# Merged semaphore clears, an earlier second-to-last expert, and context loads in four parts, in a decoder kernel of two layers

## What is computed

```
x = x + xattn0(layernorm(x), ctx, mask)     # keys with mask == 0 are left out
x = x + ffn0(layernorm(x))                  # self attention over 1024 rows, gate, top-2 router,
                                            # 8 experts 256->512->256 with a norm and gelu inside
x = x + xattn1(layernorm(x), ctx)
x = x + ffn1(layernorm(x))                  # 8 experts, each takes its 512 best of 4096 tokens;
                                            # y = W2 (silu(W1 x) * (W3 x)) * weight, added into x
```

## Time and profile before

| | us |
|---|---|
| median of 3 runs | 1932.36 (1932.31 to 1933.12) |
| the profiled execution | 1935.92 |
| its span, first to last instruction | 1934.2 |

### The profile page before, as it was taken

One profiled execution on the slowest core, in us unless ns is written; L12 is line 12 of the kernel. 1 busy time (PEld: TensorE's weight loads), 2 busy tenths in 40 slices (PEclk: granted clock), 3 DMA queues, 4 the chain that ended last, 5 costly groups with the idle time before them and its releaser, 6 DMA issues. The chain is left out here.

```text
span 1934.2 us, 29342 instructions
## 1 busy us (share of the span) xinstructions
PE 1684.8 (87%) x10227; PEld 790.7 (41%) x10228; DVE 1232.6 (64%) x2122; ACT 972.6 (50%) x1811; POOL 578.7 (30%) x637
## 2 busy tenths in 40 slices
PE   6899799899999999999999793999458996529996
PEld 4466464222222222222222472577334664225564
DVE  6444358788888888888882386566484554671221
ACT  3432245488888888888888220344275331202220
POOL 5200063243221211121112135466565000104433
PEclk9999999899999999999999895899779998759998
DMA  5000059632222222322200622122310000612542
GB/s 147 1 2 1 20 171 301 220 78 41 40 40 40 40 40 49 61 48 40 40 2 2 233 72 85 53 67 67 117 42 1 1 2 1 224 66 69 129 98 33
DMA packets 112770, 134.72 MB, mean 70 GB/s; under 512 B 18576, under 2 KB 88592, under 8 KB 112368
## 3 DMA queue, kind: packets, MB, share of 16 engines
q1 hardware_dynamic: 101920, 114.33, 21.9%
q0 software_dynamic: 9552, 17.97, 3.9%
q10 hardware_dynamic: 1152, 0.54, 0.1%
HBM read 78.60 MB, written 54.06 MB: 69 GB/s over the span
## 5 line engine op out<-in xcount | busy, mean ns | idle before, releaser
L1070 DVE TENSOR_REDUCE sa_mhalf<-sa_a 128x2 f32<-128x1024 f32 x512 | 604.1, 1220 | 84.7 <-PE sa_a L1282 82.8
L1215 ACT ACTIVATE sa_e<-sa_b 128x512 f32<-128x512 f32 x683 | 383.9, 602 | 77.1 <-PE sa_b L1315 77.1
L1325 PE MATMUL sa_b2o<-sa_e,sa_v 128*17 128x512 f32 x2048 | 269.7, 598 | 0.0
L1215 ACT ACTIVATE sa_e<-sa_b2o 128x512 f32<-128x512 f32 x341 | 205.4, 602 | 40.7 <-PE sa_b2o L1315 40.7
L1315 PE MATMUL sa_b<-sa_q,sa_k 112*128 112x512 bf16 x468 | 163.4, 388 | 2.7 <-ACT sa_e L1215 2.7
L1018 POOL TENSOR_TENSOR sa_rden<-sa_o_rows,sa_minus_one 128x16 f32<-128x16 f32 x32 | 93.0, 2907 | 178.3 <-ACT sa_o_rows L1198 178.3
L234 DVE TENSOR_REDUCE xa_mx<-xa_rows 128x16 f32<-128x1024 f32 x64 | 78.3, 1224 | 96.5 <-PE xa_rows L603 96.2
L1282 PE MATMUL sa_a<-sa_k,sa_q 48*128 48x512 bf16 x704 | 113.4, 389 | 13.2 <-DVE sa_mhalf L1070 13.2
L1007 POOL CAST sa_negm<-sa_neg 16x128 bf16<-16x128 f32 x32 | 9.4, 292 | 348.8 <-issue 339.0
L478 ACT ACTIVATE xa_pT<-xa_cols 128x1024 f32<-128x1024 f32 x64 | 62.1, 1021 | 82.5 <-PE xa_cols L635 82.5
L1315 PEld LDWEIGHTS sa_b<-sa_q,sa_k 112*128 112x128 bf16 x468 | 40.6, 97 | 151.3 <-ACT sa_e L1215 129.7
(11 more groups left out here) (344 smaller groups left out, 2950.0 us busy)
## 6 DMA issues: line engine op xcount, KB each, us to landing
k_parts<-sa_parts SPq DMA_DIRECT2D x96, 128.0 KB, 2.2
tc_w<-in_L_ffn_W SPq DMA_DIRECT2D x24, 512.0 KB
sa_q<-q_parts SPq DMA_DIRECT2D x44, 192.0 KB, 5.4
sa_k<-k_parts SPq DMA_DIRECT2D x44, 192.0 KB, 5.8
q_parts<-sa_parts SPq DMA_DIRECT2D x16, 384.0 KB
ex_xg<-expert_in SPq DMA_DIRECT2D x39, 132.0 KB
v_groups<-sp_vt SPq DMA_DIRECT2D x8, 544.0 KB, 4.7
sa_v<-v_groups SPq DMA_DIRECT2D x16, 272.0 KB, 7.4
```

The source lines that it names most:

```text
L1070: nc.vector.tensor_reduce(mhalf[a % 2][:, half, head:head + PAIRED + 1:PAIRED, t], aps[a_slot(use)][:], axis=X, op=ALU.max).then_inc(a_use ...
L1215: nc.scalar.activation(ex[(KT * n + kt) % (LAG + 1)][:, head], bps[use % 3], ACT.Exp, scale=SCALE).then_inc(b_used, 1)
L1325: last = nc.tensor.matmul(ops[32 * head:32 * head + VW], vs[s][:, kt, head], ex[(KT * n + kt) % (LAG + 1)][:, head], start=(kt == 0), stop ...
```

## The change

1. A `Kit` can be given a keeper: its semaphores' numbers go into the keeper's list and it opens no clearing block of its own. `xa0_` gives its to `c0_`, `sa_` to `sp_`, `ex_` to `at_`, `xa1_` and `c1_` to `sm_` (the scope around the self-attention layer), `sw_` and `tc_` to `x_`. `ao_`, `ts_` and `ct_` keep their own. Lists are sorted before they are cleared.
2. A context's loads: the keys' weights, the four context loads, the values' weights, the queries' weights, the two other biases; later the output's weights and `bo`. Keys, values and queries get semaphores of their own, and TensorE waits for each where it is used. In the first cross attention the mask goes behind x chunk 3 instead of behind chunk 7, and DVE's key bias, values and fill are moved. In the first cross attention, too, scores of the first chunk start one iteration earlier.
3. Expert tiles: `add_b2` runs two tiles ahead instead of one.
4. Closing experts: the outputs of expert 6 are made, weighed and scattered behind block f = 1 of expert 7's `hidden`; SP, not GpSimd, waits for the last scatters.

```diff
 class Kit:
-    def __init__(self, nc, ctx, prefix):
+    def __init__(self, nc, ctx, prefix, keeper=None):
         self.nc, self.ctx, self.prefix = nc, ctx, prefix
-        self.numbers = []
-        ctx.callback(self.clear_semaphores)
+        self.numbers = keeper.numbers if keeper else []
+        if not keeper:
+            ctx.callback(self.clear_semaphores)
...
+        self.numbers.sort()
         with self.nc.Block() as block:
...
     def issue(self, sp):
         w = self.w
-        loads = [(self.wts[:], w["wts"].rearrange("f (k p) n -> p f k n", p=P))]
...
+        def weights(f):
+            return self.wts[:, f], w["wts"][f].rearrange("(k p) n -> p k n", p=P)
...
+        self.keys_count = load(self.keys_loaded, weights(1), *[(self.ctxT[:, k, :, twice, :], w["ctxT"][k * P:(k + 1) * P])
+                                                               for twice in range(2) for k in range(HALVES)])
+        self.values_count = load(self.values_loaded, weights(2))
+        self.queries_count = load(self.queries_loaded, weights(0))
+        self.count = load(self.loaded, (self.bqk[:], w["bqk"]), (self.bv[:], w["bv"].partition_broadcast(P)))
+        self.issued = True
+
+    def issue_output(self, sp):
+        w = self.w
+        for dst, source in ((self.wts[:, 3], w["wts"][3].rearrange("(k p) n -> p k n", p=P)),
+                            (self.bo[:], w["bo"].partition_broadcast(P))):
             sp.dma_start(dst, source).then_inc(self.loaded, 16)
+        self.whole = self.count + 32
...
                         if c == 4:
                             context.issue(sp)
+                            context.issue_output(sp)
...
                         if c == 0:
                             context.issue(sp)
-                    sp.dma_start(mask_i[:], mask.rearrange("(t p) k -> p t k", p=P)).then_inc(mask_loaded, 16)
+                        if c == 3:
+                            sp.dma_start(mask_i[:], mask.rearrange("(t p) k -> p t k", p=P)).then_inc(mask_loaded, 16)
+                    context.issue_output(sp)
...
                     moments(1)
-                    place_key_bias()
                     for c in range(CHUNKS):
                         if c >= 1:
                             normalize_x(c)
-                        if c == 0:
-                            place_values()
                         if c + 2 < CHUNKS:
                             moments(c + 2)
+                        if c == 0:
+                            place_key_bias()
                         if c == 2:
+                            place_values()
+                        if c == 3:
                             place_fill()
...
-                pool.wait_ge(context.loaded, context.count)
+                pool.wait_ge(context.loaded, context.whole)
...
-                    act.wait_ge(kbias_made, 1)
                     act.wait_ge(k_psum, HALVES)
...
                         evacuate_qT(c, half)
+                    if c == 0:
+                        act.wait_ge(kbias_made, 1)
...
-                pe.wait_ge(context.loaded, context.count)
+                pe.wait_ge(context.keys_loaded, context.keys_count)
...
+                pe.wait_ge(context.values_loaded, context.values_count)
...
+                pe.wait_ge(context.queries_loaded, context.queries_count)
...
-                        if c >= CHUNKS - 2:
+                        if c >= CHUNKS - 3:
                             pe.wait_ge(qT_ready, HALVES)
-                            scores(0, c - (CHUNKS - 2))
-                    scores(0, 2)
+                            scores(0, c - (CHUNKS - 3))
                     scores(0, 3)
...
+                pe.wait_ge(context.loaded, context.whole)
                 for c in range(CHUNKS):
                     attend(c)
...
                 def body(k, turn, j, ahead):
-                    if k + 1 < MT:
-                        add_b2(k + 1, turn + (j + 1) // U, (j + 1) % U)
+                    if k + 2 < MT:
+                        add_b2(k + 2, turn + (j + 2) // U, (j + 2) % U)
...
+                add_b2(1, 0, 1)
                 turns(pool, body)
...
                     load(sp, e + 3, e % 3)
+                sp.wait_ge(scattered, 16 * CAPT * E8)
...
-                pool.wait_ge(scattered, 16 * CAPT * E8)
...
+                        if f == 1 and e + 1 == E8:
+                            outputs(e - 1)
...
-                for e in range(1, E8):
+                for e in range(1, E8 - 1):
                     hidden(e)
                     outputs(e - 1)
+                hidden(E8 - 1)
                 outputs(E8 - 1)
...
+                        if f == 1 and e + 1 == E8:
+                            weigh(e - 1)
...
-                for e in range(1, E8):
+                for e in range(1, E8 - 1):
                     gate(e)
                     weigh(e - 1)
+                gate(E8 - 1)
                 weigh(E8 - 1)
```

More of the change, by code:

```diff
@@ L84, in __init__ @@
     def __init__(self, kit, w):
-        self.w, self.loaded, self.issued = w, kit.sem("loaded"), False
+        self.kit, self.w, self.loaded, self.issued = kit, w, kit.sem("loaded"), False
+        self.keys_loaded, self.values_loaded, self.queries_loaded = (kit.sem(f"{n}_loaded") for n in ("keys", "values", "queries"))
         self.wts = kit.sb("wts", [P, 4, HALVES, D])
@@ L2501, in _, with swiglu_experts @@
                 dve.wait_ge(inverted, 1)
-def swiglu_experts(nc, ident, weights, load, w_loaded, idx, less_best, rz, gathers, x_stored, out):
+def swiglu_experts(nc, keeper, ident, weights, load, w_loaded, idx, less_best, rz, gathers, x_stored, out):
     with ExitStack() as ctx:
-        kit = Kit(nc, ctx, "sw_")
+        kit = Kit(nc, ctx, "sw_", keeper)
         sb, ps, sem = kit.sb, kit.ps, kit.sem
```

34 lines of the change are left out of this document (17 added, 17 removed).

## The result

The changed kernel took 1919.62 us (median of 4 runs, 1912.33 to 1922.00) beside 1932.74 us of the kernel before: a ratio of 0.9923, 95% interval 0.9898 to 0.9948. It is faster by 13.1 us, where 26.5 us were forecast, and 13.7 us above the forecast time.

A forecast was written before the change was run, and what follows sets the result against it. TensorE, busy 87%, was taken to bound the long stages, leaving only its holes and the boundaries; 10.3 + 9.3 + 1.0 + 1.9 + 4.0 = 26.5 us, taken from the profiled time and then 3.6 for the median, gave 1905.9 us, range 1900 to 1915.

The forecast's parts named there:

- clears and blocks: Stage boundaries: sorted, shared lists merge semaphore clears into ranges and drop six clearing blocks; 10.3 us less, bounds 8 and 11.3.
- start-up: First cross attention: reordered loads start keys and chunk 1 earlier, scores one iteration earlier; 9.3 us less, bounds 5 and 12.
- second cross attention: Its reordered loads sit behind five row loads and TensorE waits for ACT's rows anyway; 0 us, bounds -1 and +1.
- expert tiles: End of that loop: the last addition one body earlier lets GpSimd's scatters close up; 1.0 us less, bounds 0 and 2.
- closing scatters: Closing stage: expert 6's outputs inside expert 7's products let the last scatter start earlier; 1.9 us less, bounds 1.0 and 2.9.
- drain: Kernel's end: with SP waiting, GpSimd's drain ends 3.3 us behind the last scatter, not 7.3; 4.0 us less, bounds 0 and 5.1.
- Rival (a): Boundaries: clears don't merge because living semaphores' numbers lie between; only blocks go, 2.0 us instead of 10.3, giving 1914; chance 0.11.
- The mask's term: First cross attention: the 1 MB mask ahead of x chunks 4 to 7 delays chunk 4; -1.5 us, bounds 0 and -4.
- rival (b): Start-up held by loads: quarters pay fixed parts, keys land no earlier than 13.97; 5.7 us instead of 9.3, 1909.5; chance 0.12.
- Rival (c): Kernel's end: GpSimd's drain takes as long as it did; 4.0 us less gain, giving 1910; chance 0.11.
- the sign that I had set for it: Kernel's end: GpSimd's drain ending 5 us or more behind the last scatter's end, instead of 3.3, would show Rival (c).
- (d): Self-attention or closing stage: new timing lowers TensorE's clock; slower needs 53 us more low stretches, mean under 0.93; chance 0.03.

The follow-up runs named there:

- number 3: The kernel before with only the changed loads of the two contexts, their waits, and DVE's and TensorE's order in start-up: 1925.83 us (5 runs), ratio 0.9959.
- number 8: The changed kernel with the last wait for the scatters' landing on GpSimd again instead of SP: 1918.35 us (4 runs), ratio 0.9929.

## Why the prediction was wrong

**By its terms.** Measured is the difference of the means over all traces with and without the edit:

```
term                      forecast   measured
clears and blocks           10.3       9.6    (14.6 - 5.0; number 3 has 14.8)
start-up                     9.3       8.4    (233.4 in 5 traces, 225.0 in 12)
second cross attention       0        -4.4    (241.4 in 4 traces of it without the edit or hold;
                                               245.3, 249.6, 241.3, 247.0 of the changed kernel)
expert tiles                 1.0       1.8    (177.1 in 6, 175.3 in 11)
closing scatters             1.9       1.7    (190.3 in 5, 188.65 in number 8)
drain                        4.0       2.3    (188.65 in number 8, 186.3 in 10)
sum                         26.5      19.4
```

The remaining four stages add 0.4 or less either way. Over four occasions the kernel before had medians of 1932.2 to 1933.8 us and the changed one 1919.6, 1917.5, 1911.8 and 1913.5; all 16 runs of it have a median of 1914.9, some 18 us below before.

**Clears and blocks: right.** I counted 8 clears in 8 blocks and there are 14, with the long ranges at 0.18 to 0.37 us: 0.7 us less. Rival (a) is out.

**Start-up: right in place, and in size partly by luck.** Keys at 11.46 (forecast 11.7), chunk 1's transposes at 18.31 (19.4), transposed maxima at 67.07 (65.4) instead of 74.73; the stage 9.3 us shorter in the trace after and 8.4 in the mean. Up to the maxima the gain was 7.7 us, not 9.3. By TensorE's chunks it is 7.5 for the start of chunk 1 (forecast 6.4) and 3.0 for its work at 2.4 GHz (3.0), then -4.0 for the mask (-1.5): 2.3 us of them until chunk 3 starts, and 1.7 for its projection, 5.29 us instead of 3.60 at the lower clock. One round less behind the loop, with its products inside it, gives 1.2 (1.4). The mask's term was thus the mis-sized one; the last 1.6 us of the stage's 9.3 came behind the maxima, where the trace of before has 3.4 us at 1.2 GHz, from 76.2 on, and the trace after none. The three transfers more didn't run one by one, so rival (b) is out: the second x landed at 13.61 (forecast 13.5) instead of 15.44. The Trainium skill's wish for transfers of at least 1 MiB ("DMA: Bandwidth & Descriptors", section "Bandwidth") had no price here that the trace shows; the page's figures are for loads that GpSimd issues, and these are SyncE's. The part of the term that the clock gives back is not sure: the 12 traces lie between 222.5 (0 us at 1.2 GHz) and 226.5 us (6.8).

**Second cross attention: the step that failed.** "I take 0; bounds -1 and +1" looked only at what the edit does to this stage's loads. But two engines stood within 0.3 us of each other there: copy at 1469.31, first addition at 1469.57, as the rows above show, and I hadn't read them. In their place the runs showed a hold of two VectorE operations that costs the stage 3.1 to 4.6 us, in three of four traces of the changed kernel, and in the mean of the four, with the clock's own scatter in it, 4.4 us. Which side an execution falls on hangs on the clock of the projection ahead and, at 5.3 us, on the last 0.3 us. The price was there to be read too, in the start-up of the trace of before, where the last normalization stands beside the same additions:

```profile
39.45 1.34 DVE L224 TENSOR_SCALAR xa_xn<-x_x,xa_mv,xa_rstd 128x256 f32<-128x256 f32 x4
...
43.72 18.93 POOL L373 TENSOR_TENSOR x_x<-x_x,c_bo 128x1024 f32<-128x1024 f32 x8
47.22 8.60 DVE L224 TENSOR_SCALAR xa_xn<-x_x,xa_mv,xa_rstd 128x256 f32<-128x256 f32 x4 [0.89 <-PE xa_front L569]
```

Four instructions, 8.60 us instead of 1.34. A bound of one or two additions, 2.3 to 4.6 us, would have followed from it.

**Expert tiles: right in size.** The 1.8 us contain time at 1.2 GHz: the two slowest traces without the edit, 178.5 and 178.6 us, have 18 us of it. Of the traces without the edit, four have 12.3 to 12.5 us of it and took 176.2 to 176.4 us; with the edit it is 11.1 to 11.8 us and the stage 174.9 to 175.6. That is 1.0 us, of which up to 0.5 is still the clock's. The edit wasn't run by itself.

**Closing stage: the order right, the drain mis-sized.** The reordering gave 1.7 of 1.9 us. The drain ends 5.0 us behind the last scatter, not 3.3: the row that I took (the expert tiles) was the nearest of its kind and still another case. The 4.94 us that the drain took by itself in the closing stage was the row to use: 7.3 - 4.9 = 2.4. Rival (c), that nothing is gained, is out too, although the sign that I had set for it, a gap of 5 us or more, is met: the sign was wrong, since the gap was 7.3 us before.

**From the profile to the median: a constant that isn't one.** I forecast 1909.4 us for a profiled execution and 1912.33 was measured, 2.9 off, while the median was 13.7 off. I had taken the 3.6 us between the profile of before and its median over to the changed kernel, whose profile lay 7.3 us under its median. The near hit of the profile is luck: a slow draw of before against a fast one of after. Taking over the 3.6 us is the same as taking 26.5 us from the median of before, so it is no cause of its own. The 13.7 us are 26.5 - 19.4 = 7.1 in the terms above, the largest being the second cross attention; 1919.6 - 1914.9 = 4.7 between the first four executions, whose median is the highest of four occasions, and all 16; and 1.9 that the traces don't account for.

The kernel before scatters over 1928 to 1938 us, the changed one over 1907 to 1922, and the granted clock goes with it (0.943 at 1907.5, 0.936 at 1921.0). Two things are seen to differ between its four traces: the hold, which three have and one hasn't, and the stretches at 1.2 GHz, 218 to 233 us in total inside the stages. Which of them takes an execution to 1922 isn't shown: the three above 1918 us have no trace.

**The range.** The bounds of the parts, added up, are 13.0 and 34.3 us, not the 17 to 31 that I wrote and took 1900 to 1915 from. The 13.1 us measured lie at their very edge.

**Slower, by the clock (d):** no; the clock rose from 0.936 to 0.941.

## What to carry to other kernels

When an edit shifts a stage in time without touching it, look in that stage for a VectorE copy or other small operation on SBUF that starts within a few tenths of a microsecond of a long GpSimd operation, and price the other order. Here a GpSimd addition of 2.3 us beside a copy of 0.25 us fell on either side from one execution to the next, with TensorE's clock ahead of the copy. Long GpSimd work that is wanted much later can stand behind a wait on the operations that it could hold. And a profile is one draw: before the sum is taken over to a median, its own place in the spread is unknown by several microseconds, and the range should say so on both sides.

## What the runs showed of the hardware

- A VectorE copy (128 x 128) or a scalar-tensor-tensor on four columns beside GpSimd additions of 2.31 us ends with the addition in progress: 0.25 and 0.15 us become up to 2.41 and 2.32. Beside a memset of 0.53 us they take 0.54 and 0.40. Reductions of PSUM (1.22 us) are not held.
- In the closing stage GpSimd's drain ends 5.0 us behind the last indirect scatter, adding or writing, and takes 4.94 us when all have landed before it starts; in the expert tiles it ends 3.3 us behind; the landing of an adding scatter is 2.3 us behind its end on the engine, of a writing one 1.4.
- A range clear takes 0.044 us for a few numbers and up to 0.37 for a long range; a clear on its own costs 0.071 us with its issue.
- The same program showed 218 to 233 us at 1.2 GHz inside its stages from one execution to the next, and 1907 to 1922 us of time. The granted clock of one projection (3.60 or 5.3 us) moved VectorE's copy by 1.7 us against GpSimd's additions.
